# A Flamingo block with a routed FP4 expert layer: the down products by a lead scale per column

## The reference

```python
w = FP4_LUT[codes] * jnp.repeat(scales, 128, axis=-2)      # dequant_fp4
x = x + tanh(g_xattn) * (0.6 * sigmoid(si + sj + b) + 0.4 * layernorm(x))
h = layernorm(x)
probs = softmax(h @ gate_w.T); vals, idx = top_k(probs, 4); w = vals / sum(vals)
act = swiglu(h @ w_gu[e])            # 512 -> 2 x 384, then silu(gate) * up
out = sum_e combine[t, e] * (act @ w_d[e])   # 384 -> 512
out = out + swiglu(h @ shared_gu) @ shared_d
x = x + tanh(g_ffn) * out
```

## Time and profile before

| | |
|---|---|
| median of 3 runs | 685.47 us (684.33 to 687.44) |
| the profiled execution | 684.48 us |
| its span, first to last instruction | 682.7 us |
| TensorE busy | 628.4 us (92%) |
| VectorE busy | 489.0 us (72%) |
| GpSimd busy | 327.3 us (48%) |
| ScalarE busy | 325.1 us (48%) |
| mean granted TensorE clock | 0.982 of 2.4 GHz |
| DMA | 93.72 MB, mean 137 GB/s |

### The profile page before, as it was taken

One profiled execution on the slowest core, in us unless ns is written; L12 is line 12 of the kernel. 1 busy time (PEld: TensorE's weight loads), 2 busy tenths in 40 slices (PEclk: granted clock), 3 DMA queues, 4 the chain that ended last, 5 costly groups with the idle time before them and its releaser, 6 DMA issues.

```text
span 682.7 us, 17258 instructions
## 1 busy us (share of the span) xinstructions
PE 628.4 (92%) x4394; PEld 381.3 (56%) x4395; DVE 489.0 (72%) x1271; ACT 325.1 (48%) x558; POOL 327.3 (48%) x506
## 2 busy tenths in 40 slices
PE   3769879999998999999999999999999999999992
PEld 2445456566554565665655565665656555656650
DVE  6998879892876767687878676788678787766210
ACT  1765477331344444544554554545455454545441
POOL 3522844001235565654655655555654646556422
PEclk9999989999999999999999999999999999999996
DMA  8770112046176685847768675766958678554432
GB/s 233 217 235 17 48 62 93 2 117 247 33 212 160 152 213 102 201 93 199 155 148 208 120 192 112 183 136 158 206 113 187 120 195 186 108 94 75 82 48 31
DMA packets 49841, 93.72 MB, mean 137 GB/s; under 512 B 8840, under 2 KB 16776, under 8 KB 49816
## 3 DMA queue, kind: packets, MB, share of 16 engines
q0 software_dynamic: 16128, 38.35, 30.6%
q1 hardware_dynamic: 32936, 55.04, 27.2%
q10 hardware_dynamic: 752, 0.04, 0.1%
HBM read 65.16 MB, written 28.24 MB: 137 GB/s over the span
## 4 chain that ended last, share of the span: by engine, by line
PE 81%; DVE 7%; DMA 3%; ACT 3%; issue 2%; POOL 2%; SPq 1%; DVEq 0%; POOLq 0%; ACTq 0%
PE gu_ps L1211 45%; PE bank L1239 22%; PE bank L1251 4%; PE bank L1225 4%; DMA dn_sc<-dn_scale_halves 2%; PE bank L1266 1%; DMA room_a<-in_ctx 1%; DVE stats L728 1%; PE gu_ps L1171 1%; PE bank L1168 1%; PE bank L1195 1%; POOL room_a L462 1%; DVE X L1005 1%; ACT xT L572 1%; DVE X L760 1%
## 5 line engine op out<-in xcount | busy, mean ns | idle before, releaser
L1211 PE MATMUL gu_ps<-wgu,mix_room 128*128 x1728 | 304.4, 326 | 2.9 <-DVE tick L955 1.6
L1211 PEld LDWEIGHTS gu_ps<-wgu,mix_room 128*128 128x128 f16 x1728 | 166.0, 98 | 114.2 <-issue 7.6
L1239 PE MATMUL bank<-wdn,aT 128*128 (+1 forms) x792 | 186.8, 381 | 3.3 <-ACT aT L632 2.1
L533 POOL DMA_INDIRECT out<-mix_room,idx_s x72 | 123.2, 1711 | 31.9 <-issue 29.5
L632 ACT ACTIVATE aT<-bank 128x768 f16<-128x768 f16 x88 | 71.2, 809 | 140.3 <-PE bank L1225 135.4
L1239 PEld LDWEIGHTS bank<-wdn,aT 128*128 128x128 f16 x792 | 77.5, 98 | 89.0 <-issue 4.9
L504 POOL TENSOR_TENSOR pool_tick<-ones 128x1 f32<-128x1 f32 x144 | 36.3, 252 | 164.6 <-DMA out<-mix_room,idx_s 85.5
L996 DVE SCALAR_TENSOR_TENSOR act<-gu_ps,wslot,sg x72 | 44.5, 618 | 96.4 <-ACT sg L618 82.9
L625 ACT ACTIVATE acth<-act 128x384 f16<-128x384 f32 x88 | 46.0, 523 | 120.7 <-DVE act L996 120.7
L515 POOL DMA_INDIRECT room_b<-token_rows,idx_g x72 | 76.5, 1063 | 12.0 <-issue 3.1
L512 POOL COPY idx_g<-room_b 128x1 int32 (+1 forms) x72 | 42.2, 586 | 67.9 <-DVE tick L866 46.2
(11 more groups left out here) (157 smaller groups left out, 587.3 us busy)
## 6 DMA issues: line engine op xcount, KB each, us to landing
dn_sc<-dn_scale_halves SPq DMA_DIRECT2D x34, 384.0 KB
dn_raw<-in_L_ffn_down_packed SPq DMA_DIRECT2D x48, 256.0 KB
gu_sc<-gu_scale_halves SPq DMA_DIRECT2D x34, 192.0 KB
X<-in_x SPq DMA_DIRECT2D x4, 1024.0 KB, 8.0
token_rows<-room_a SPq DMA_DIRECT2D x16, 256.0 KB, 2.0
out<-X SPq DMA_DIRECT2D x4, 1024.0 KB, 10.7
gu_raw<-in_L_ffn_gate_up_packed SPq DMA_DIRECT2D x16, 192.0 KB
gu_raw<-in_L_ffn_gate_up_packed SPq DMA_DIRECT2D x16, 191.9 KB
```

The source lines that it names most:

```text
L533: nc.gpsimd.indirect_dma_start(out[:, :], bass.IndirectOffsetOnAxis(idx_s[:, b:b + 1], 0), y_sb[:, b, :], None, compute_op=ALU.add).then_i ...
L1211: mm = nc.tensor.matmul(ps[b][:, 0:I], x(xp * HC + c), wgu[:, w, wp, c, col:col + I], start=(c == 0 and xp == 0 and wp == 0), stop=(c == H ...
L1239: mm = nc.tensor.matmul(y_ps[0 if shared else b][:, :], aT[:, b, ap, t, :], wdn[:, w, wp, t, :], start=(n == 0), stop=(n == 3 * IC - 1))
```

## The change

Each column of an expert's down weights gets a lead scale, and the scales of the three groups of rows are divided by it. The lead is the first group's scale, raised by powers of two where the others have larger exponents. The first group's ratio is then exact in one float16 part, so its low part is neither stored nor loaded, VectorE does not make its low weights, and a routed slot has eight down products. The y of a slot is multiplied by the lead scales of its expert on GpSimd before it is added to the output. The shared expert stays as it was.

What moves with it:

- SyncE does not load the routed down scales at the start but later, as three loads behind the first expert's words; VectorE finds leads (six and nine instructions on 64 columns) and ratios (six on 192 columns) behind slots 4 and 5 of the shared stage; SyncE stores them (six stores) behind the row store of tile 11, waits for them, and loads the first expert's ratios and two experts' leads; VectorE waits for these (`ld_lead`) at slot 6. The further leads are loaded with each expert, 256 KB.
- GpSimd's `add(s)` waits for the gate and up products of slot s+2 (`gu_done`), multiplies, waits for the product and then scatters. The last two adds do not wait for `gu_done`.
- The copy of gather indices goes to ScalarE (`list_ahead`), three slots ahead.

```diff
-                sp.dma_start(dn_sc[:, buf, hl, :, :],
-                             dn_s_dram[hl, n].unsqueeze(0).broadcast_to([P, IC, H])).then_inc(ld_w[buf], 16)
+        def load_dn_scales(sp, buf, n, landed):
+            for hl in range(2):
+                t0 = 0 if hl == 0 or (isinstance(n, int) and n == 0) else 1
+                sp.dma_start(dn_sc[:, buf, hl, t0:, :],
+                             dn_s_dram[hl, n, t0:].unsqueeze(0).broadcast_to([P, IC - t0, H])).then_inc(landed, 16)
...
             for i in range(NT):
 
+                if i == 12:
+                    sp.wait_ge(dn_split, 1)
+                    for hl in range(2):
+                        for t in range(hl, IC):
+                            sp.dma_start(dn_s_dram[hl, 1:, t, :].rearrange("e (b n) -> e b n", n=HB),
+                                         dn_h[:, hl, t, :]).then_inc(st_dn, 16)
+                    sp.dma_start(lead_dram.rearrange("e (b n) -> (e b) n", n=HB), lead_s[:, :]).then_inc(st_dn, 16)
+                    sp.wait_ge(st_dn, 16 * (2 * IC - 1 + 1))
+                    load_dn_scales(sp, 1, 1, ld_lead)
+                    for n in (1, 2):
+                        load_lead(sp, n, ld_lead)
...
             def add(s, b):
+            def add(s, b, lock_step=True):
 
                 pool.wait_ge(st_out, 16 * (B + 1))
+                both = pool.value_load(others_i[0:1, bass.ds(s, 1)], min_val=16 * E, max_val=8 * SLOTS * E + E - 1)
+                others, e = both // E, both % E
                 if not isinstance(s, int) or s >= 2:
                     pool.wait_ge(added[b], 8 * (s - b))
                 nc.gpsimd.tensor_copy(idx_s[:, b:b + 1], tok[:, bass.ds(s, 1)]).then_inc(idx_s_ready, 1)
+                pool.wait_ge(yev_done, s + 1)
+                if lock_step:
+                    pool.wait_ge(gu_done, s + NT + 3)
+                nc.gpsimd.tensor_tensor(y_out[:, b, :], y_sb[:, b, :],
+                                        lead_y[:, bass.ds(e, 1), :].rearrange("p k n -> p (k n)"), ALU.mult).then_inc(y_scaled, 1)
...
                 pool.wait_ge(idx_s_ready, s + 1)
+                pool.wait_ge(y_scaled, s + 1)
+                hold_wait(6 + b)
+                nc.gpsimd.indirect_dma_start(out[:, :], bass.IndirectOffsetOnAxis(idx_s[:, b:b + 1], 0), y_out[:, b, :],
                                              None, compute_op=ALU.add).then_inc(added[b], 16)
...
+            def list_ahead(s, b):
+
+                nc.scalar.activation(idx_g[:, b:b + 1], tok_room[:, bass.ds(s, 1)], ACT.Copy).then_inc(idx_g_ahead, 1)
...
+            def lead_exponents():
+
+                EXPONENT, TINY, DEEP = 0x7F800000, 2.0 ** -100, 2.0 ** -20
+                v.wait_ge(ld_dn, 16 * IC)
...
+            def lead_scales():
...
+                step(nc.vector.reciprocal(inv, own), wait=False)
+                step(nc.vector.tensor_scalar(lead_s[:, :], own, 1.0 / W_SCALE, None, ALU.mult))
+
+            def down_ratios():
+
+                step(nc.vector.tensor_tensor(dn_all, dn_all, inv.unsqueeze(1).broadcast_to([P, IC, HB]), ALU.mult))
...
                 if i == 4:
                     attend(3)
                     second_stats(3)
+                    lead_exponents()
+                    lead_scales()
                 if i == 5:
+                    down_ratios()
                     first_weights(0)
                 if i == 6:
+                    v.wait_ge(ld_lead, 64)
                     first_weights(1)
...
                     for hl in range(2):
+                        skip = 0 if hl == 0 or shared else max(0, H - d * COLS)
+                        if skip >= COLS:
+                            continue
...
-                for t in range(IC):
-                    for ap, wp in ((0, 0), (0, 1), (1, 0)):
+                terms = [(t, ap, wp) for t in range(IC) for ap, wp in ((0, 0), (0, 1), (1, 0))
+                         if shared or t or not wp]
+                for t, ap, wp in terms:
```

More of the change, by code:

```diff
@@ L272, in gated_xattn_moe @@
         st_out = sem("st_out")
+        y_scaled = sem("y_scaled")
+        idx_g_ahead = sem("idx_g_ahead")
+        ld_lead = sem("ld_lead")
+        ld_dn = sem("ld_dn")
+        dn_split = sem("dn_split")
+        st_dn = sem("st_dn")
         st_rows = [sem(f"st_rows{k}") for k in range(ROWS_AHEAD)]
@@ L360, in _ @@
             for part, done in ((0, st_sc_sh), (1, st_sc)):
-                for k, dram in ((part, gu_s_dram), (2 + part, dn_s_dram)):
+                for k, dram in ((part, gu_s_dram), (2 + part, dn_s_dram))[:2 - part]:
                     for hl in range(2):
@@ L647, in take_y @@
                 if not isinstance(r, int) or r >= 2:
-                    a.wait_ge(added[b], 8 * (r - b))
-                nc.scalar.activation(y_sb[:, b, :], y_ps[b][:, :], ACT.Copy, scale=1.0 / W_SCALE).then_inc(yev_done, 1)
+                    a.wait_ge(y_scaled, r - 1)
+                nc.scalar.activation(y_sb[:, b, :], y_ps[b][:, :], ACT.Copy).then_inc(yev_done, 1)
             for i in range(2):
@@ L679, in _, with slot @@
             inner = a.value_load(pairs_i[0:1, 0:1], min_val=E // 2 - 2, max_val=SLOTS // 2 - 2)
-            def slot(r, b, rows=True):
+            def list_ahead(s, b):
+                nc.scalar.activation(idx_g[:, b:b + 1], tok_room[:, bass.ds(s, 1)], ACT.Copy).then_inc(idx_g_ahead, 1)
+            def slot(r, b, rows=True, ahead=True):
                 copy_aT(r + (NT - 1), 1 - b)
@@ L684, in slot @@
                     take_rows(r + 1, 1 - b)
+                if ahead:
+                    list_ahead(r + 3, 1 - b)
                 activate(NT + r, b)
@@ L692, in _ @@
                 slot(2 * j + 1, 1)
-            slot(2 * inner + 2, 0)
-            slot(2 * inner + 3, 1, rows=False)
+            slot(2 * inner + 2, 0, ahead=False)
+            slot(2 * inner + 3, 1, rows=False, ahead=False)
             copy_aT(2 * inner + 3 + NT, 1)
@@ L722, in _ @@
                                          ALU.logical_shift_left), wait=False)
+            s0, s1, s2 = (dn_all[:, t, :] for t in range(IC))
+            e_rest, e_lead, reach, keep, up, own, other, inv = (lead_room[:, k, :] for k in range(8))
+            def lead_exponents():
+                EXPONENT, TINY, DEEP = 0x7F800000, 2.0 ** -100, 2.0 ** -20
+                v.wait_ge(ld_dn, 16 * IC)
+                step(nc.vector.tensor_scalar(e_rest.bitcast(I32), s1.bitcast(I32), EXPONENT, None, ALU.bitwise_and), wait=False)
+                step(nc.vector.tensor_scalar(up.bitcast(I32), s2.bitcast(I32), EXPONENT, None, ALU.bitwise_and), wait=False)
+                step(nc.vector.tensor_scalar(e_lead.bitcast(I32), s0.bitcast(I32), EXPONENT, None, ALU.bitwise_and))
+                step(nc.vector.scalar_tensor_tensor(e_rest, e_rest, TINY, up, ALU.max, ALU.max))
+                step(nc.vector.scalar_tensor_tensor(keep, e_rest, DEEP, e_lead, ALU.mult, ALU.is_le), wait=False)
+                step(nc.vector.scalar_tensor_tensor(reach, e_rest, DEEP, e_lead, ALU.mult, ALU.max))
@@ new lines, in lead_scales @@
+            def lead_scales():
+                step(nc.vector.reciprocal(up, reach), wait=False)
+                step(nc.vector.tensor_scalar(other, keep, -1.0, 1.0, ALU.mult, ALU.add))
+                step(nc.vector.tensor_tensor(up, up, e_rest, ALU.mult), wait=False)
+                step(nc.vector.tensor_tensor(other, other, e_rest, ALU.mult))
+                step(nc.vector.scalar_tensor_tensor(own, up, 1.0, s0, ALU.max, ALU.mult))
+                step(nc.vector.tensor_tensor(own, own, keep, ALU.mult))
+                step(nc.vector.tensor_tensor(own, own, other, ALU.add))
+                step(nc.vector.reciprocal(inv, own), wait=False)
+                step(nc.vector.tensor_scalar(lead_s[:, :], own, 1.0 / W_SCALE, None, ALU.mult))
```

120 lines of the change are left out of this document (79 added, 41 removed).

## The result

| | before | after |
|---|---|---|
| median, 4 runs each | 685.75 us | 721.46 us (715.72 to 722.63) |
| ratio after/before, 95% interval | | 1.0503 (1.0471 to 1.0535) |
| the profiled execution | 684.48 us | 720.83 us |
| its span | 682.7 us | 718.7 us |

The direction was forecast, the size was not: +36 us where I had worked out +9, and above the range. First the page of the changed kernel: busy times, the clock's row over forty slices, and the chain of waits by engine and by line.

A forecast was written before the change was run, and what follows sets the result against it. TensorE alone was taken to bound the routed stage, VectorE level with it in four-slot experts; -15.7 + 3.5 + 12 + 4.2 + 4.5 + 1.2 - 0.5 = +9.2 us on 684.48 gave 693.7, left at 694; range 673 to 705.

The forecast's parts named there:

- The gain of the ninth product: Routed stage, TensorE: eight down products for nine in 72 slots, 0.216 us each, at most 15.7 us gained.
- The later gather: GpSimd's queue: gather behind the new wait late by 0.7 us in six five-slot experts, 4.2 us lost.
- The set-up: Shared stage: VectorE waits near 105 us for the scale loads; cost 4.5 us, bounds 1.5 and 10.
- spread over an expert: Expert loads: 128 KB more per expert, counted as nothing.
- the multiply's sum: GpSimd's multiply blocking VectorE, 3.5 us in five-slot and 12 in four-slot experts, plus 1.2 us bare at the end.
- 3.5 + 12 + 1.2: Multiply: seven five-slot experts 3.5 us, eight four-slot experts 12 us, bare multiply before the last scatter 1.2 us.
- relative to the full 15.7: Four-slot experts give back between 0.4 and 2.2 us each of the down products' gain; 1.5 taken, 12 us for eight.
- VectorE's sum over a round: Four-slot experts: VectorE's round of 27.60 us loses 0.45 and gains up to 1.8, between 27.15 and 28.95 us.
- The first rival: Routed stage: multiply falls in VectorE's pause, gathers land in 6.2 us; 676.5 us, between 671 and 681; chance 0.27.
- the other case: Set-up stores of 128 B pieces land like scale stores, 2 us later; sum would be 2 us more.
- The third rival: Routed stage: an expert's first scatter waits for the previous expert's last, landing in 8.9 us; 705 us and more; chance 0.10.
- The front: Ahead of the context on SyncE: one scale load less, 0.5 us gained.

The follow-up runs named there:

- both orders: Changed kernel with the gather ahead of the add in GpSimd's queue and VectorE's wait for the first ratios late and narrow: 701.47 us; multiply on 8 columns: 683.87 us.
- part 9: Kernel before: eight products and fewer low weights 675.80 us; slot counts read early, VectorE's loop written out 679.71; that with eight products 668.68. Repaired changed kernel 682.89.
- experiments 2 and 5: Multiply cut to 8 of 512 columns: in the changed kernel 698.93 us; with gather ahead of add and VectorE's wait late 683.87, against 701.47 with whole multiply.
- experiment 6: Changed kernel with gather ahead of add and VectorE's wait late, plus ScalarE's index copy moved ahead of its copy of the transposed rows: 690.78 us.
- experiments 3 and 5: Changed kernel with the gather ahead of the add: 709.41 us; with VectorE's wait for the first ratios late and narrow as well: 701.47 us.
- experiment 8: Kernel before with only the ninth product of each routed slot left out: 675.84 us; with only GpSimd's wait for the gate and up products added: 688.79 us.
- experiment 2: Changed kernel with the multiply by the lead cut to 8 of 512 columns, all waits kept: 698.93 us.
- experiment 7: On the 690.78 us kernel (gather, VectorE's wait, index copy moved): gu_half copy behind the fourth slot's low half, 698.47 us; then leads on their own semaphore, 698.61 us.

## Why the prediction failed

I forecast +9.2 us with four costs against a gain of 15.7, and measured +36. Four steps of the sum failed. The gain of the ninth product was charged in full, -15.7 us, and was 9.4. The later gather was put at 4.2 us and cost 11.6. The set-up was put at 4.5 us and cost 8.4. And 8.1 us came with the rest of the change, which the sum had at about nothing; half of it stands at the start of the routed stage, where the load of a lead comes late that I had held to be "spread over an expert". Only the multiply's sum came out, in part by luck.

The runs give a ladder from the kernel before to the changed one, each step a difference of two medians:

| step | us |
|---|---|
| kernel before | 685.4 |
| eight products alone | -9.4, to 675.8 (forecast -15.7) |
| the change with both orders mended, multiply on 8 columns | +8.1, to 683.9 |
| whole multiply | +17.6, to 701.5 (forecast 3.5 + 12 + 1.2) |
| gather behind the add | +11.6, to 713.1 (forecast 4.2) |
| VectorE's wait early and for all four loads | +8.4, to 721.5 (forecast 4.5) |

*Down products: the largest error of thought.* I wrote that "the most that this can give is 15.7 us" and then charged all of it. In the same text I read that four-slot experts take 27.60 us where TensorE alone takes 26.5, so that they had no time to give; I put that into the multiply's term, as the loss "relative to the full 15.7": 0.41 us of each four-slot expert's 1.5, 3.3 us in all, so my forecast for eight products alone was really -12.4 us. It was also the wrong bound: I worked with VectorE's sum over a round (27.15 us), and the runs of part 9 show that this sum does not bind, but one stretch with 1.21 us of the reading and register steps behind it. The four-slot steps gave 0.14 us for 0.86. The product 0.216 us itself was right.

*The multiply's blocking: right in kind, in its sum partly by luck.* 16.7 us forecast (13.4 without those 3.3), 17.6 measured, with the mechanism that the earlier trace rows had shown: VectorE's instruction and the multiply do not overlap. The first rival, by which VectorE's pause covers the whole multiply, is refuted by experiments 2 and 5. But the 17.6 us were measured in the kernel of both orders, where the multiply comes late and hits dq_sign in every decoding slot, while gu_half takes its 0.56 us. That is not the place that I had priced. In the changed kernel it is: there gu_half is hit, and seven four-slot experts wait 13.8 us for high halves (3.3 us in three before). With the multiply moved near that place (experiment 6) the kernel lies only 6.9 us above the one with 8 columns (690.78 and 683.87); that one was not run with the index copy early, so the multiply's price there stays open.

*The gather: mechanism right, size three times too small.* It takes 4.6 us from issue to landing at the median, within the 6.2 us I gave it, but TensorE waited in 13 places, up to 2.3 us, not in six by 0.7. I had let it hide in the waits after four-slot experts; of the 16.6 us of waits, experiments 3 and 5 show 12 as not hidden by anything. The wait alone made 4.4 us of such waits in the kernel before and cost 3.5 us (experiment 8). With the multiply on 8 columns 10.6 of the 16.6 us of waits were still there (experiment 2), so the multiply's length made only 6.0 of them; what raises 4.4 to 10.6 (shorter slots, the index copy behind ScalarE's other work, a second register read) was not taken apart.

*The set-up: both halves under-priced.* The loads landed at 112.7 us, not at 110.6. The six stores took 0.64 us of issue each (3.20 us for five), not 0.43. Each landed in 1.9 to 2.3 us, the lead's in 1.7, quicker than my 2.5, and SyncE issued the next load 1.2 us behind the last store's issue (104.89 to 106.05). The loads took 4.9 us behind the last issue (107.82 to 112.7), not 3. The Trainium skill (DMA: Bandwidth & Descriptors, "Specifications") says that transfers under 512 B are read, modified and written, from which I had 2 us more as the other case; these stores in pieces of 128 B landed like the row stores (2.0 us), not like the scale stores (4.6). And I gave lost time only its own length: at 121.98 us twelve products took 3.05 us for 2.11, at a granted clock of 0.59 from 118.8 to 125.1 us.

*Hardly in the sum.* The 8.1 us of the second step, where the sum had 1.5 us for the set-up's instructions and -0.5. Some 4 us of it stand at the start of the routed stage, where the output stores and an expert's load meet: up to there the first kernel below is 1.4 us ahead of the second (207.81 and 209.20), one slot later 2.7 us behind it (224.71 and 221.96). The kernel of both orders with the small multiply, and then the kernel before with eight products:

```profile
212.94 0.56 DVE L1069 COPY gu_half<-gu_raw 128x768 uint16<-128x768 uint16 x1 [6.51 <-DMA xT<-dn_lead_scales]
...
217.14 4.05 PE L1333 MATMUL gu_ps<-wgu,mix_room 128*128 x12
```

```profile
212.21 0.58 DVE L950 COPY gu_half<-gu_raw 128x768 uint16<-128x768 uint16 x1 [4.54 <-DMA dn_sc<-dn_scale_halves]
...
215.75 2.11 PE L1211 MATMUL gu_ps<-wgu,mix_room 128*128 x12
```

VectorE waits 2.0 us more, for the lead, and TensorE's twelve products behind its own longer wait (5.77 us for 3.66) take 4.05 us for 2.11, at a granted clock of 0.50 from 215.7 to 221.0 us. So "counts as nothing, since it is spread over an expert" failed for this load. A semaphore of its own for the lead gave nothing measurable back all the same (experiment 7), on a kernel whose runs spread over 7 us; what it would give by itself stays open. From there to the last group of down products the two kernels differ by another 0.6 us, and then by 2.7 us in the tail. There the second kernel's last eight products ran at full clock and the first one's at 0.54:

```profile
664.77 3.58 PE L1362 MATMUL bank<-wdn,aT 128*128 x8 [1.05 <-ACT aT L697]
```

```profile
661.47 1.90 PE L1240 MATMUL bank<-wdn,aT 128*128 x8 [1.04 <-ACT aT L632]
```

That is no property of the change: the kernel before took 3.59 us for its nine. Against the kernel before the tail of the changed one, from its last down products to the end, is 15.3 us for 14.7 (703.44 of 718.7, 668.01 of 682.7), within the 1.2 us that I had for the multiply. The profiled executions differ by 6.2 us in all, so 1.9 of the 8.1 us lie between executions. The front gained nothing for its one load less: the products that stood at 59.81 us stand at 59.76.

The third rival, the scatter as the wait, did not come: from 225 to 640 us GpSimd was idle 84 us for the products and only 5 us for landed scatters (78.6 before).

## What to carry to other kernels

A saving on the bounding engine counts only where that engine is the bound: split the loop by its cases (here four and five slots) and multiply by those alone. When a wait is added to an in-order queue, first look what stands behind it that does not need it, and put that ahead; here that was worth 12 us, and a wait moved to its first use 8 us. "issue" time between two instructions of an engine can be the bound as well: reading a count into a register in the middle of a tight stretch cost 5 us in all, which came back when it was read earlier and the loop was written out.

## What the runs showed of the hardware

A GpSimd product on 512 columns makes VectorE's instruction wait even when the latter starts at nearly the same time and takes one input from SBUF: dq_sign, 0.36 us alone, took 1.45 us when it started 0.05 us behind the multiply. The Trainium skill (SBUF — State Buffer, "Who interferes with whom") states that whoever starts first holds the shared ports for the whole instruction, and the rows agree. It frees VectorE's instructions with one SBUF input of this unless they run in a two-port mode, and lists copies and tensor_scalar, the kinds of gu_half's copy and dq_sign, among those that can; no row tells in which mode they run. VectorE's activation product, which reads PSUM, kept its mean of 0.616 to 0.618 us in the kernels with the multiply, also without the wait for the products; at 409.85 us in experiment 6's last kernel it took 0.62 us in the midst of a multiply (409.62, 1.27 us).

With the gathers on time, moving ScalarE's index copy brought the multiply from 1.71 us behind the start of the down products (412.07 and 410.36) to 1.05 (409.62 and 408.57), and gave 10.7 us over 72 slots.
